# Graph network on one core: loop bounds loaded four at a time, and index checks at run time left out

## What is computed

```
x = _layernorm(x + _L0_gnn_ref(...))   # three relational convolutions
x = _layernorm(x + _L1_gnn_ref(...))   # attention over edges
x = _layernorm(x + _L2_gnn_ref(...))   # weighted sum of neighbours
x = _layernorm(x + _L3_gnn_ref(...))   # mean of edge features, two dense layers
...
def rgcn_conv(x, src, dst, etype, W, root, bias):
    seg = dst * R + etype
    agg = jax.ops.segment_sum(x[src], seg, num_segments=n * R)
    cnt = jax.ops.segment_sum(jnp.ones((src.shape[0],), x.dtype), seg, num_segments=n * R)
    agg = jnp.where(cnt[:, None] > 0, agg / jnp.maximum(cnt, 1.0)[:, None], 0.0).reshape(n, R, -1)
    return jnp.einsum('nrd,rdk->nk', agg, W) + x @ root + bias
```

## Time and profile before

| | us |
|---|---|
| time, median of 3 runs | 6167.65 |
| lowest, highest | 6163.09, 6174.96 |
| span of the profiled execution, first to last instruction | 5385.6 |
| median less that span | 782.05 |
| TensorE matmuls busy | 4150.9 |
| GpSimd busy | 3014.2 |
| VectorE busy | 2954.1 |
| ScalarE busy | 964.9 |

### The profile page before, as it was taken

The page is one execution under the profiler, slowest core; times in us unless marked ns, Lnnn a source line. Parts: engine busy times, 40 slices in busy tenths (PEclk is TensorE's granted clock), DMA queues, the critical chain, the costliest instruction groups (busy, mean ns, idle before and its releaser), DMA issues.

```text
span 5385.6 us, 98227 instructions
## 1 busy us (share of the span) xinstructions
PE 4150.9 (77%) x20763; PEld 2938.9 (55%) x20764; DVE 2954.1 (55%) x6694; ACT 964.9 (18%) x3611; POOL 3014.2 (56%) x3064
## 2 busy tenths in 40 slices
PE   4777677778888788888878788887766988898863
PEld 1223265666666555555545555555665766676652
DVE  5444333333322677777777777877893333333335
ACT  0111111111111111111211111112441111111112
POOL 0000066666665677777767777775005777777750
PEclk7678778777777999999999999999785555656666
DMA  2011233333344222222322222322442333333320
GB/s 73 27 44 49 74 97 115 120 115 120 117 123 124 74 71 71 85 92 94 105 89 71 71 82 88 95 94 85 148 157 83 104 103 102 101 103 103 101 71 12
DMA packets 318265, 492.02 MB, mean 91 GB/s; under 512 B 98090, under 2 KB 221228, under 8 KB 314556
## 3 DMA queue, kind: packets, MB, share of 16 engines
q0 software_dynamic: 108864, 246.74, 16.0%
q1 hardware_dynamic: 209372, 244.94, 13.7%
HBM read 406.11 MB, written 85.29 MB: 91 GB/s over the span
## 4 chain that ended last, share of the span: by engine, by line
PE 30%; DMA 26%; issue 19%; POOL 12%; DVE 8%; DVEq 2%; ACT 2%; POOLq 1%; ACTq 0%; SPq 0%
DMA msg_r<-y_tab,idx_r 21%; POOL msg_r L494 12%; PE psum L1452 6%; DMA msg_r<-z_tab,idx_r 4%; PE psum L1387 4%; PE psum L1597 3%; PE psum L1598 2%; PE psum L1267 1%; PE psum L1279 1%; DVE hot_r L983 1%; DVE h_t L1142 1%; PE psum L1549 1%; PE psum L1399 1%; PE psum L1414 1%; PE psum L1299 1%
## 5 line engine op out<-in xcount | busy, mean ns | idle before, releaser
L494 POOL DMA_INDIRECT msg_r<-y_tab,idx_r x2160 | 2163.1, 1001 | 1561.7 <-issue 1185.3
L1452 PE MATMUL psum<-shot_r,hotb_r 128*128 128x400 bf16 x5760 | 1221.9, 335 | 359.2 <-DMA msg_r<-y_tab,idx_r 318.9
L494 POOL DMA_INDIRECT msg_r<-z_tab,idx_r x882 | 844.4, 957 | 630.8 <-issue 584.8
L1452 PEld LDWEIGHTS psum<-shot_r,hotb_r 128*128 128x128 bf16 x5760 | 480.3, 98 | 760.4 <-DMA msg_r<-y_tab,idx_r 404.0
L1007 DVE TENSOR_SCALAR shot_r<-iota_h,edge_g 128x1600 bf16<-128x1600 f16 x1440 | 893.6, 675 | 0.0
L570 ACT COPY idx_r<-row_i 128x1 int32 x2142 | 410.0, 191 | 2456.9 <-DMA msg_r<-y_tab,idx_r 2337.2
L1597 PE MATMUL psum<-msg_r,shot_r 128*128 128x128 f32 x1764 | 636.3, 460 | 143.7 <-DMA msg_r<-z_tab,idx_r 107.3
L1387 PE MATMUL psum<-hot_r,msg_r 128*128 128x128 f32 x2880 | 575.0, 358 | 194.3 <-DMA msg_r<-y_tab,idx_r 101.1
L1387 PEld LDWEIGHTS psum<-hot_r,msg_r 128*128 128x128 f32 x2880 | 486.5, 253 | 300.6 <-DMA msg_r<-y_tab,idx_r 158.3
L1597 PEld LDWEIGHTS psum<-msg_r,shot_r 128*128 128x128 f32 x1764 | 414.3, 292 | 339.2 <-DMA msg_r<-z_tab,idx_r 284.9
L1598 PE MATMUL psum<-msg_r,hot_r 128*128 128x128 f32 x1764 | 521.9, 396 | 0.0
(11 more groups left out here) (276 smaller groups left out, 3795.1 us busy)
## 6 DMA issues: line engine op xcount, KB each, us to landing
msg_r<-in_attr SPq DMA_DIRECT2D x882, 64.0 KB
h_t<-count_tab SPq DMA_DIRECT2D x25, 1600.0 KB, 6.5
count_tab<-w_s SPq DMA_DIRECT2D x48, 800.0 KB, 3.7
msg_r<-y_tab,idx_r POOLq DMA_INDIRECT x2160, 2.7
xn<-heavy_tab SPq DMA_DIRECT2D x76, 320.0 KB
y_tab<-y_s SPq DMA_DIRECT2D x25, 640.0 KB, 2.9
xn<-y_tab SPq DMA_DIRECT2D x25, 640.0 KB, 4.1
y_tab<-y_s SPq DMA_DIRECT2D x50, 320.0 KB
```

The source lines that it names most:

```text
L494: pool.indirect_dma_start(out=msg_r[:, q, 0:width], out_offset=None, in_=table, in_offset=bass.IndirectOffsetOnAxis(ap=idx_r[:, q:q + 1], ...
L1452: ins = T.matmul(psum[:, 4 + b, 0:CB], hotb_r[:, q, :], shot_r[:, q, b * CB:(b + 1) * CB], start=first, stop=last)
```

## The change

The tables are turned so that the field is the fast index, `tile_ranges` loads all four fields of a tile by one TENSOR_LOAD into four registers, and P0, P1 and LAST are masked with 0xFFFFF (a register operation each). An unused field's mask isn't emitted. CHUNK, and all column and slot numbers derived from it, carry no check at run time.

```diff
-        groups, rest = sb("groups", [1, 4, 32], I32), sb("rest", [1, 4, 32], I32)
-        windows = sb("windows", [1, 4, 32], I32)
+        groups, rest = sb("groups", [1, 32, 4], I32), sb("rest", [1, 32, 4], I32)
+        windows = sb("windows", [1, 32, 4], I32)
...
+        def bounded(x, lo, hi, why):
+            return nc.s_assert_within(x, lo, hi, skip_runtime_bounds_check_because=why)
+        numbers = count(1)
+        def tile_ranges(eng, D, of=groups):
+            at = slice(D, D + 1) if type(D) is int else bass.ds(D, 1)
+            row = [eng.alloc_register(name=f"row{next(numbers)}") for _ in range(4)]
+            eng.load(row, of[0:1, at, :].rearrange("a b c -> a (b c)"))
+            got = []
+            for n, r in enumerate(row):
+                if n == CHUNK:
+                    got.append(eng.snap(r, min_val=-MOST, max_val=MOST))
+                else:
+                    kept = eng.alloc_register(name=f"kept{next(numbers)}")
+                    eng.reg_alu(kept, r, MASK, op=ALU.bitwise_and)
+                    got.append(eng.snap(kept, min_val=0, max_val=MOST))
+                    eng.free_register(kept)
+            for r in row:
+                eng.free_register(r)
+            return got
         def tile_range(eng, what, D, of=groups):
-            return eng.value_load(of[0:1, what, bass.ds(D, 1)])
+            return tile_ranges(eng, D, of)[what]
...
+        MOST, MASK = CHUNKS * WN, 0xFFFFF
         def first_chunk(eng, c):
-            return eng.snap(c, min_val=0, max_val=COLS - U)
+            return bounded(eng.snap(c), 0, COLS - U, "a group's chunks are among those of the edges")
...
                 with act.Fori(begin + 1, TILES - 1) as D:
-                    first, last = tile_range(act, P0, D, tab), tile_range(act, LAST, D, tab)
-                    rows_to_gather(k, of, D, first, last, tab)
-                    rows_to_gather(k, of, D + 1, last, last + 1, tab)
+                    first, _, chunk, last = tile_ranges(act, D, tab)
+                    rows_to_gather(k, of, chunk, first, last)
+                    rows_to_gather(k, of, tile_range(act, CHUNK, D + 1, tab), last, last + 1)
...
             with dve.Fori(0, TILES) as D:
-                p0, p1, chunk = (tile_range(dve, n, D) for n in (P0, P1, CHUNK))
+                p0, p1, chunk = tile_ranges(dve, D)[:3]
...
-                        slot = dve.snap(v % VD, min_val=0, max_val=VD - 1)
+                        slot = bounded(dve.snap(v % VD), 0, VD - 1, "it is a remainder")
...
                 with pe.Fori(w0, w1) as w:
-                    v0, v1 = (tile_range(pe, n, w, windows) for n in (P0, P1))
+                    v0, v1 = tile_ranges(pe, w, windows)[:2]
...
                 def tile(D, slot):
-                    first, last = pe.snap(tile_range(pe, P0, D, tab)), pe.snap(tile_range(pe, LAST, D, tab))
+                    first, _, _, last = tile_ranges(pe, D, tab)
```

More of the change, by code:

```diff
@@ L10 @@
 from contextlib import ExitStack
+from itertools import count
 import numpy as np
@@ L429, in _ @@
             with sp.Fori(0, TILES) as D:
[L430 removed]
+                p0, p1, chunk = tile_ranges(sp, D)[:3]
                 with sp.Fori(p0, p1) as p:
@@ L558, in _, with rows_to_gather @@
             n_groups, n_rest = tile_range(act, LAST, TILES - 1), tile_range(act, LAST, TILES - 1, rest)
-            def rows_to_gather(k, of, D, before, end, tab):
-                chunk = tile_range(act, CHUNK, D, tab)
+            def rows_to_gather(k, of, chunk, before, end):
                 with act.Fori(before, end) as b:
@@ L593, in gathering @@
                     flush(D)
-                rows_to_gather(k, of, TILES - 1, tile_range(act, P0, TILES - 1, tab), tile_range(act, LAST, TILES - 1, tab), tab)
+                first, _, chunk, last = tile_ranges(act, TILES - 1, tab)
+                rows_to_gather(k, of, chunk, first, last)
                 if table is not None:
@@ L921, in _ @@
                 with dve.Fori(w0, w1) as w:
-                    v0, v1, off = (tile_range(dve, n, w, windows) for n in (P0, P1, CHUNK))
+                    v0, v1, off = tile_ranges(dve, w, windows)[:3]
                     with dve.Fori(v0, v1) as v:
-                        c = dve.snap(v + off, min_val=0, max_val=COLS - 1)
-                        slot = dve.snap(v % VD, min_val=0, max_val=VD - 1)
+                        c = bounded(dve.snap(v + off), 0, COLS - 1, "a block's chunks are among those of the edges")
+                        slot = bounded(dve.snap(v % VD), 0, VD - 1, "it is a remainder")
                         alone(dve)
@@ L971, in _ @@
             with dve.Fori(1, TILES) as D:
-                p0, p1, chunk = (tile_range(dve, n, D, rest) for n in (P0, P1, CHUNK))
+                p0, p1, chunk = tile_ranges(dve, D, rest)[:3]
                 with dve.Fori(p0, p1) as p:
@@ L1023, in counting @@
                 dve.sem_inc(s_go, 1)
-                one_hots_and_sources(k, 1, dve.snap(tile_range(dve, P0, 1, rest)), tile_range(dve, CHUNK, 1, rest))
+                first, _, chunk, _ = tile_ranges(dve, 1, rest)
+                one_hots_and_sources(k, 1, first, chunk)
                 with dve.Fori(1, TILES - 1) as D:
-                    first, end, chunk = (tile_range(dve, n, D, rest) for n in (P0, P1, CHUNK))
+                    first, end, chunk = tile_ranges(dve, D, rest)[:3]
                     with dve.Fori(first + 1, end) as p:
@@ L1030, in counting @@
                         after_tile(D)
[L1031 to L1034 removed]
+                    first, _, chunk, _ = tile_ranges(dve, D + 1, rest)
+                    one_hots_and_sources(k, D + 1, first, chunk, lambda: counts_out(k, D))
+                first, _, chunk, _ = tile_ranges(dve, TILES - 1, rest)
+                with dve.Fori(first + 1, p_end) as p:
                     one_hots_and_sources(k, TILES - 1, p, chunk)
```

26 lines of the change are left out of this document (11 added, 15 removed).

## The result

The change makes the kernel **faster by 153 us, 2.5%**: 6012.43 us (median of 4, 6009.65 to 6015.82) against 6165.37 (median of 4, 6162.8 to 6174.96); the ratio on record is 0.9745, with a 95% interval of 0.9731 to 0.9759. A second set of runs gave 0.9743 (0.9715 to 0.9771). I had forecast 6125 us, 43 us less, and even my lower end (6080) was too high.

A forecast was written before the change was run, and what follows sets the result against it. TensorE's sequencer was taken to bound the first stage's loop over groups and GpSimd passes 1 to 3. Terms -24 (first stage), -15 (pass 0) and -4 (passes 1 to 3) summed to -43 us, 6125 us; range 6080 to 6165.

The forecast's parts named there:

- first stage -24: First stage: 33 us saved in the loop over groups and 9 us lost on the loads, together -24 us.
- I take 33: First stage, TensorE's loop over groups: removed checks save 26 to 39 us, only where the sequencer isn't ahead; 33 taken.
- 0.35 us per group: First stage, TensorE's loop over groups: one comparison, two assertions and three gaps removed save 0.35 us in each of 147 groups.
- L: Time of one load of four registers, taken as 0.75 us, between the ends 0.30 and 1.2.
- quick-load rival: A load of four is as quick as one (0.30 us), giving 6094 us; chance 0.27.
- the loads' term: First stage, loads at tile and window starts: -2 us for tiles and +11.5 for windows, +9 together.
- VectorE loses the same checks: First stage, VectorE: losing its checks costs or brings nothing by itself, since TensorE hardly waits for it.
- matmuls rival: First stage: checks go but matmuls take over as the bound, perhaps with more time at the lower clock; 6160 us, chance 0.07.
- I take this part as unchanged: The 782.05 us by which the median of the runs exceeds the profiled span was assumed to stay the same.
- Pass 0 (-15): Pass 0: 15 of the 19.4 us that TensorE's transpose L1318 waits for VectorE go, bounds -19 and -8.
- passes 1 to 3 (-4): Passes 1 to 3: -4 us from GpSimd's waits for ScalarE's row numbers, bounds -20 and +50.
- slower rival: Passes 1 to 3: ScalarE's second long load at tile boundaries becomes GpSimd's wait; 6212 us, chance 0.08.

The follow-up runs named there:

- groups_free: The control without checks in the first stage's two loops over groups, on TensorE and VectorE; 6140.14 us, 0.9959 of before.
- rows_only: The changed kernel with the checked snap back and CHUNK's register unbounded, so four-field loads and masks but all checks; 6049.69 us, 0.9938 of before.
- masked_before: The control: the kernel before with a mask behind each single load of P0, P1 and LAST, nothing else changed; 6106.15 us, 1.0028 of before.
- tensor_first: The control with the changed first stage on TensorE alone; 5355.41 us, 0.9992 of before.
- before_5_9: The control with 9 slots for visits and 5 for groups (5 and 8 before); 5391.91 us, 1.0058 of before.
- passes_only: The change in the passes and the stages behind them alone, first stage as in the control; 5347.77 us, 0.9985 of before.
- after_again: The changed kernel once more, unaltered, beside other runs on their chip; 6012.73 us, 0.9743 of before.
- first_stage: The control with the changed first stage on both VectorE and TensorE, passes as in the control; 5979.77 us, 0.9803 of before.
- slots_5_9: The changed kernel with 9 slots for visits and 5 for groups (5 and 8 before); 5217.70 us, 0.9735 of before.
- slots_6_7: The changed kernel with 7 slots for visits and 6 for groups; 5227.32 us, 0.9763 of before.
- no_zeros: The changed kernel without the matmul of zeros in TensorE's loop over visits (191 matmuls); 6036.85 us, 0.9788 of before.
- check_back: The changed kernel with the check on the group's column back in TensorE's first-stage loop over groups; 5246.72 us, 0.9778 of before.
- the pair with 9 and 5 slots: The changed kernel with 9 visit and 5 group slots, with and without the matmul of zeros per visit; 0.9735 and 0.9815 of before.

## Why the prediction was wrong

The direction, the stage that gains most and the size of the passes' sum were right. The sum fell short by 110 us, 94 of them in the term "first stage -24", which was 118. The two parts that the forecast priced there came to 52 us (33 forecast) and, by the measured load, to 14 (9 the other way). The other 52 us lie in what it put at nothing: VectorE's checks, and the clock.

- **"It shows at least in the 74 idle pieces of the matmuls and hardly in more than the 110 of the weight loads, ... I take 33."** The 0.35 us per group was right (0.36 in `groups_free`), but it came to what all 147 groups hold, 52 to 53 us. Where matmuls were still in the array, the loop's pace was the sequencer's all the same.
- **"No row is nearer to one end, so I take the middle, 0.75."** L was 0.33 on TensorE (0.31 to 0.34 above). The quick-load rival named it. With 0.33 in the forecast's own sum the loads' term is -14 and not +9 (-12 for the tiles, -2 for the windows). `rows_only` brought the first gather 46 us sooner than in the control, whose masks come on top: 25 us of it lie in the tables (121.9 us against 147.2), 13 as idle time ahead of L1292 (48.9 to 35.9) and 10 as shorter matmuls there (93.4 to 83.8). What the Trainium skill states on the page "Runtime: NRT & Kernel Launch", section "Instruction fetch mechanics" (about 200 ns for each register, in bulk too), doesn't agree with these rows: three more registers cost 30 to 36 ns together. The page speaks of loads from HBM, these are from SBUF.
- **"VectorE loses the same checks ... That costs or brings nothing by itself, since TensorE hardly waits for it."** This is the step of the mechanism that failed. The 18.5 us of waiting in the earlier trace rows are what is left while TensorE is slow itself. `tensor_first` shows what comes up once it isn't: 45.1 us. One engine's change was worth 34 and 32 us, both 133.
- **The matmuls rival had the clock's sign wrong.** I argued that more work per time might bring more time at the lower level. The clock rose from 0.76 to 0.92, and the matmuls of the tables of tiles 1 to 24 alone, from a table's first start to its last end, fell from 103.5 to 81.2 us. I had no term for a gain by the clock.
- **"I take this part as unchanged"**, of 782 us outside the span: there is no such part. It did no harm to the difference, but it hid that the passes I read were those of another chip.
- Pass 0 (-15) and passes 1 to 3 (-4): 20 us against before, 23 against the control (10 to 36). That the sum fits is in part luck. In pass 0 the wait named is gone and 11 us came out; passes 1 to 3, which were to keep their lengths within 5 us each, lost 2, 17 and 5, and the source that I had for them didn't give it. The slower rival, ScalarE's second long load, had nothing to work with at 0.31 us a load.

By the two given traces, the 118 us are groups -52, tables -31, visits and window starts -28, and the rest -6. How much of each is clock can't be told apart by one number. The tables' matmuls take 91 to 104 us in four traces with the old stage (before, `masked_before`, `before_5_9`, `passes_only`) and 75 to 83 in five with the changed one (after, `after_again`, `first_stage`, `slots_5_9`, `slots_6_7`), so the 22 us of the given pair could as well be 8 or 29. `no_zeros` shows that a clock lower by 0.22 goes with a stage longer by 38.

## What to carry to other kernels

When two engines feed each other through a few slots, relieve both and price both: the small wait in a profile can be the difference of two slow engines, and not what the second one costs. In loops of short matmuls count sequencer instructions, since checks that cost 0.2 to 0.35 us here were paid in every round, and four bounds that lay side by side were fetched by one load at little more than the price of one. Before subtracting anything from a trace, compare its span with the times that it is to explain.

## What the runs showed of the hardware

- Chips differ by 14 to 15% on this kernel: 5356 to 5360 us on three, 6091 and 6168 on two. On the slow kind GpSimd stalls for 2.6 us at a time in the passes: in pass 3 of after 83 times, mostly 9 gathers apart, and 50 times in the control's, mostly 9 or 18 apart, but never in pass 3 of before, `check_back` or `passes_only` on the quick kind. A gather itself takes about the same 0.94 us on both. GpSimd in pass 3 of after, then of `check_back` on the quick kind:

```profile
4607.39 0.94 POOL L519 DMA_INDIRECT msg_r<-z_tab,idx_r  x1 [0.30 <-issue]
4608.64 0.95 POOL L519 DMA_INDIRECT msg_r<-z_tab,idx_r  x1 [0.30 <-issue]
4612.20 1.20 POOL L519 DMA_INDIRECT msg_r<-z_tab,idx_r  x1 [2.61 <-ACT idx_r L593]
```

```profile
4406.10 0.94 POOL L519 DMA_INDIRECT msg_r<-z_tab,idx_r  x1 [0.30 <-PE psum L1623]
4407.34 0.94 POOL L519 DMA_INDIRECT msg_r<-z_tab,idx_r  x1 [0.30 <-issue]
```

  Why, stays open: the change doesn't touch it, and no run was made on it. It is also open whether the chips differ or something in their state.
- Four registers by one load cost 309 to 344 ns against 279 to 308 for one.
- A table's nine matmuls take 2.96 us at a granted clock of 1.0 and 5.70 at 0.5.
- 191 matmuls of zeros that add nothing to the sums and no time to their own loop are worth 38 us in the first stage, with the granted clock at 0.92 instead of 0.70 (42 us in the pair with 9 and 5 slots).
